# Gram matrices of a pairwise-attention kernel in two parts of 32 rows on eight tiles of TensorE

## What is computed

```
row, col = triu_indices(39, k=1)                 # 741 pairs of fields
ip     = x[:, row, :] * x[:, col, :]             # (B, 741, 64)
hidden = relu(ip @ W_w + b_w)                    # (B, 741, 64)
logits = hidden @ W_h + b_h                      # (B, 741)
a      = softmax(logits, axis=1)
y      = (sum over pairs of a * ip) @ W_p + b_p  # (B, 1)
```

## Time and profile before

| | us |
|---|---|
| median of 3 runs (1036.34 to 1036.84) | 1036.56 |
| the profiled execution | 1036.49 |
| its span in the profile | 1034.7 |
| PE busy | 1023.2 (99%) |
| DVE busy | 980.4 (95%) |
| ACT busy | 872.6 (84%) |
| POOL busy | 402.7 (39%) |

### The profile page before, as it was taken

One profiled execution on the slowest core, in us unless ns is written; L12 is line 12 of the kernel. 1 busy time (PEld: TensorE's weight loads), 2 busy tenths in 40 slices (PEclk: granted clock), 3 DMA queues, 4 the chain that ended last, 5 costly groups with the idle time before them and its releaser, 6 DMA issues.

```text
span 1034.7 us, 58749 instructions
## 1 busy us (share of the span) xinstructions
PE 1023.2 (99%) x24849; PEld 486.7 (47%) x24849; DVE 980.4 (95%) x550; ACT 872.6 (84%) x885; POOL 402.7 (39%) x326
## 2 busy tenths in 40 slices
PE   8999999999999999999999999999999999999997
PEld 3445454454544545454454544545445454454542
DVE  8999999999999999999999999999999999999992
ACT  6888888888888888888888888888888888888885
POOL 3644555333334333343424334233343333433331
PEclk9999999999999999999999999999999999999999
DMA  3242242422324133241421414214232242422312
GB/s 53 36 50 48 36 51 47 50 36 48 41 43 58 27 55 41 36 62 29 56 44 27 62 35 50 47 31 55 44 41 47 36 49 47 46 39 45 41 35 27
DMA packets 330745, 45.33 MB, mean 44 GB/s; under 512 B 330715, under 2 KB 330731, under 8 KB 330731
## 3 DMA queue, kind: packets, MB, share of 16 engines
q1 hardware_dynamic: 330411, 45.10, 30.7%
q10 hardware_dynamic: 320, 0.07, 0.0%
HBM read 26.59 MB, written 18.54 MB: 44 GB/s over the span
## 4 chain that ended last, share of the span: by engine, by line
PE 97%; DVE 2%; DMA 0%; issue 0%; ACT 0%; DVEq 0%; ACTq 0%
PE z L517 62%; PE logits L570 31%; PE z L506 5%; DVE prod L345 2%; DMA first_x_rows<-in_r_x_dram 0%; DVE x_wide L316 0%; PE logits L558 0%; DVE neg_max L354 0%; DVE weighted L362 0%; ACT exps L453 0%; PE z L497 0%; DVE x_wide L319 0%; DVE x_scaled L320 0%; PE z L640 0%; DVE x_wide L327 0%
## 5 line engine op out<-in xcount | busy, mean ns | idle before, releaser
L430 ACT ACTIVATE hidden<-z,b_col 128x988 f32<-128x988 f32 x768 | 803.9, 1084 | 132.2 <-PE z L517 127.5
L345 DVE TENSOR_TENSOR prod<-x_wide 128x2964 f32<-128x2964 f32 (+1 forms) x257 | 821.2, 3243 | 1.0 <-issue 0.2
L517 PE MATMUL z<-prod,w_tiles 64*32 64x494 f32 x12288 | 761.1, 576 | 1.4 <-DVE prod L345 0.7
L284 POOL COPY head_w<-head_cols 128x64 f32<-128x64 f32 x252 | 354.7, 1411 | 559.2 <-PE logits L570 559.2
L570 PE MATMUL logits<-hidden,head_w 64*32 64x371 f32 (+1 forms) x8192 | 440.6, 471 | 0.4 <-PE logits L570 0.4
L517 PEld LDWEIGHTS z<-prod,w_tiles 64*32 64x32 f32 x12288 | 260.5, 106 | 247.8 <-issue 223.0
L570 PEld LDWEIGHTS logits<-hidden,head_w 64*32 64x32 f32 x8192 | 179.8, 106 | 244.5 <-issue 229.2
L316 DVE STREAM_TRANSPOSE x_wide<-x_rows 128x1024 f32<-128x1024 f32 x63 | 78.4, 1245 | 24.5 <-PE z L506 20.9
L506 PEld LDWEIGHTS z<-x_wide,x_scaled 64*39 64x39 f32 x4096 | 44.8, 113 | 39.5 <-issue 39.5
L438 ACT COPY gram_out<-z 103x624 f32<-103x624 f32 x64 | 44.3, 692 | 17.4 <-PE z L506 17.4
L291 POOL COPY gram_out<-gram_out 103x304 f32<-103x304 f32 x64 | 39.4, 615 | 46.8 <-ACT gram_out L438 46.8
(11 more groups left out here) (29 smaller groups left out, 26.5 us busy)
## 6 DMA issues: line engine op xcount, KB each, us to landing
gram<-gram_out SPq DMA_DIRECT2D x256, 70.7 KB
x_rows<-in_r_x_dram SPq DMA_DIRECT2D x252, 64.0 KB
values<-gram SPq DMA_DIRECT2D x128, 46.3 KB, 3.5
x_rows<-in_r_x_dram SPq DMA_DIRECT2D x252, 14.0 KB
first_x_rows<-in_r_x_dram SPq DMA_DIRECT2D x2, 78.0 KB
first_x_rows<-in_r_x_dram SPq DMA_DIRECT2D x1, 156.0 KB
w_tiles<-in_L_rec_W_w_dram ACTq DMA_DIRECT2D x4, 16.0 KB, 2.8
head_cols<-in_L_rec_W_h_dram SPq DMA_DIRECT2D x4, 0.2 KB, 2.3
```

The costliest lines, as they stand in the source:

```text
L284: nc.gpsimd.tensor_copy(head_w[:, step % BLOCK_STEPS, :, :], head_cols[:, :, at:at + TILE]).then_inc(head_w_ready, 1)
L345: nc.vector.tensor_tensor(out, one, other, ALU.mult).then_inc(ready, 1)
L430: nc.scalar.activation(hidden[:, i, :, CHUNK * k:CHUNK * (k + 1)], z[:, slot_of(j), :, 0:CHUNK], ACT.Relu, bias=b_col[:, 0:1]).then_inc(z_ ...
L517: last = nc.tensor.matmul(z[col:col + TILE, slot_of(j), b, 0:CHUNK], w_tiles[row:row + D, col:col + TILE], prod[row:row + D, i, first:firs ...
```

## The change

The Gram matrix of an item is computed in two matmuls of 32 stationary columns in place of one of 39. Part 0 takes fields 0 to 31 as rows and columns 1 to 38 of x_wide; of it rows 0 to 19 are used. Part 1 takes fields 7 to 38 as rows and columns 20 to 57 of x_wide (which run over into the repeated fields); of it rows 13 to 31 are used, which are fields 20 to 38. With these two windows every row already has the columns that its pairs need, so nothing has to be repeated in `gram_out`. The eight tiles of 64 x 32 are the same as those of the chunks. A block then has 64 Gram matmuls of 38 columns in place of 32 of 39. ACT's copy takes all 128 partitions with 608 elements in place of 103 with 624. POOL's copy and the semaphore for it go, and SP waits for ACT's copy itself. In DRAM the rows have 38 entries; SP writes them in 8 DMAs a block, for u, h and part, in place of 4. The DVE memset of a corner of z at the start goes too, with TensorE's wait for it.

```diff
+    GCOLS = FIELDS - 1
+    CROSS_ROWS = FIELDS // 2 + 1
+    GRAM_PARTS = ((0, 1, 0, CROSS_ROWS, 0),
+                  (FIELDS - TILE, CROSS_ROWS, CROSS_ROWS - (FIELDS - TILE), FIELDS - CROSS_ROWS,
+                   CROSS_ROWS * GCOLS + CROSS_ROWS - 1))
+    GRAM_BATCH = FIELDS * GCOLS + CROSS_ROWS
...
-        gram_out = sb("gram_out", [P, 2, 2, ROW_DUOS, WIDE])
+        gram_out = sb("gram_out", [P, 2, 2, ROW_DUOS, GCOLS])
...
-        GRAM_DMAS = 4
+        GRAM_DMAS = 8
...
             def write_gram(v, slot):
-                sp.wait_ge(gram_wrapped, v + 1)
+                sp.wait_ge(z_read, ITEMS * v + place("gram") + 1)
                 for u in range(2):
                     for h in range(2):
-                        at = (h ^ u) * D
-                        sp.dma_start(gram_blocks[h, u, :, bass.ds(v, 1), :, :],
-                                     gram_out[at:at + FIELDS, slot, u, :, :]).then_inc(gram_written[slot], 16)
+                        for part, (_, _, skipped, rows, base) in enumerate(GRAM_PARTS):
+                            at = (h ^ u) * D + part * TILE + skipped
+                            first = gram_blocks[h, u, base:base + 1, bass.ds(v, 1), :]
+                            lines = bass.AP(first.tensor, first.offset, [[GCOLS, rows], first.ap[-1], [1, GCOLS]])
+                            sp.dma_start(lines, gram_out[at:at + rows, slot, u, :, :]).then_inc(gram_written[slot], 16)
...
                         bands = bass.AP(first.tensor, first.offset,
-                                        [first.ap[0], [WIDE + 1, FIELDS], [1, OFFSETS]])
+                                        [first.ap[0], [GCOLS + 1, FIELDS], [1, OFFSETS]])
...
-            def wrap_gram(v):
-
-                pool.wait_ge(z_read, ITEMS * v + place("gram") + 1)
-                rows = gram_out[0:ROWS, v % 2, :, :, :].rearrange("p u d w -> p (u d) w")
-                nc.gpsimd.tensor_copy(rows[:, :, FIELDS:WIDE], rows[:, :, 0:OFFSETS]).then_inc(gram_wrapped, 1)
...
-            nc.vector.memset(z[TILE:D, GRAM_SLOT, 0, QUADS * FIELDS:XCOLS], 0.0).then_inc(z_cleared, 1)
...
-                nc.scalar.copy(gram_out[0:ROWS, slot, :, :, 0:FIELDS],
-                               z[0:ROWS, GRAM_SLOT, :, 0:XCOLS].rearrange("p u (d f) -> p u d f", f=FIELDS)
+                nc.scalar.copy(gram_out[:, slot, :, :, :],
+                               z[:, GRAM_SLOT, :, 0:ROW_DUOS * GCOLS].rearrange("p u (d f) -> p u d f", f=GCOLS)
                                ).then_inc(z_read, 1)
...
             def gram_matrices(v):
                 for d in range(ROW_DUOS):
-                    for u in range(2):
-                        for h in range(2):
-                            row, col, duo = h * D, (h ^ u) * D, u * ROW_DUOS + d
-                            last = nc.tensor.matmul(z[col:col + FIELDS, GRAM_SLOT, u, FIELDS * d:FIELDS * (d + 1)],
-                                                    x_scaled[row:row + D, duo, :], x_wide[row:row + D, duo, 0:FIELDS],
-                                                    start=True, stop=True, tile_position=(row, col))
+                    for part, (field, column, _, _, _) in enumerate(GRAM_PARTS):
+                        for u in range(2):
+                            for h in range(2):
+                                row, col, duo = h * D, (h ^ u) * D + part * TILE, u * ROW_DUOS + d
+                                last = nc.tensor.matmul(z[col:col + TILE, GRAM_SLOT, u, GCOLS * d:GCOLS * (d + 1)],
+                                                        x_scaled[row:row + D, duo, field:field + TILE],
+                                                        x_wide[row:row + D, duo, column:column + GCOLS],
+                                                        start=True, stop=True, tile_position=(row, col))
                 last.then_inc(z_ready, 1)
...
-            pe.wait_ge(z_cleared, 1)
```

More of the change, by code:

```diff
@@ L107, in bass_pairwise_attention_pooling @@
     x_rows_dram = x.rearrange("(v p h) f (e d) -> h e f v p d", v=BLOCKS, h=2, e=2)
-    gram = nc.dram_tensor("gram", [BATCHES, FIELDS, WIDE], fp32, kind="Internal").ap()
-    gram_blocks = gram.rearrange("(v u p h) i w -> h u i v p w", h=2, v=BLOCKS, u=2)
-    gram_rows = gram.rearrange("(t q h) i w -> h q t (i w)", h=2, q=QUADS)
+    gram = nc.dram_tensor("gram", [BATCHES, GRAM_BATCH], fp32, kind="Internal").ap()
+    gram_blocks = gram.rearrange("(v u p h) w -> h u w v p", h=2, v=BLOCKS, u=2)
+    gram_rows = gram.rearrange("(t q h) w -> h q t w", h=2, q=QUADS)
     y_rows_dram = y.rearrange("(g c) o -> g (c o)", g=GROUPS)
@@ L155, in bass_pairwise_attention_pooling @@
         x_rows_zeroed = sem("x_rows_zeroed")
-        z_cleared = sem("z_cleared")
         w_loaded = sem("w_loaded")
@@ L170, in bass_pairwise_attention_pooling @@
         x_scaled_ready = sem("x_scaled_ready")
-        gram_wrapped = sem("gram_wrapped")
         gram_written = [sem(f"gram_written{i}") for i in range(2)]
@@ L229, in load_values @@
                         at = 32 * q + GROUP_STEPS * h
-                        first = gram_rows[h, q, bass.ds(GROUP_STEPS * g, GROUP_STEPS), 1:2]
+                        first = gram_rows[h, q, bass.ds(GROUP_STEPS * g, GROUP_STEPS), 0:1]
                         bands = bass.AP(first.tensor, first.offset,
-                                        [first.ap[0], [WIDE + 1, FIELDS], [1, OFFSETS]])
+                                        [first.ap[0], [GCOLS + 1, FIELDS], [1, OFFSETS]])
                         sp.dma_start(values[at:at + GROUP_STEPS, 0:PAIRS].rearrange(
@@ L296, in _ @@
                 nc.gpsimd.tensor_copy(head_w[:, step, :, :], head_cols[:, :, at:at + TILE]).then_inc(head_w_ready, 1)
-            wrap_gram(0)
             for step in range(BLOCK_STEPS, STEPS):
-                if step % BLOCK_STEPS == BLOCK_STEPS - 1:
-                    wrap_gram(step // BLOCK_STEPS)
                 place_heads(step)
```

## The result

The changed kernel takes 1063.86 us (median of 4 runs, 1063.15 to 1066.6) against 1036.7 before: 27.2 us more, ratio 1.0268 (95% interval 1.0256 to 1.028). The forecast was 1057.8 in a range of 1048 to 1067. The profiled execution took 1063.15 with a span of 1061.4, 26.7 more than before's 1034.7.

What follows compares the result with a forecast made beforehand. TensorE's own stream was taken as the bound (PE busy 99%). A loss of 0.335 us a block, vanished gaps included, gave 64 x 0.335 = +21.4 on 1036.49, so 1057.9, stated as 1057.8 us, range 1048 to 1067.

Steps and rivals of the forecast that it cites:

- The gaps go: Idle time around a block's Gram matrices, where TensorE changes tile size, vanishes: -0.31 us a block.
- A matmul each 0.0167 us: Hand-over limit: TensorE gets one float32 matmul each 0.0167 us at best, read from seven chunk matmuls behind `open_logits`.
- The window's limit of 0.0173: About 16 matmuls queued or under way in TensorE, each counted until complete: 0.277 / 16 = 0.0173 us a matmul.
- The last tile: Last tile of the chunk after the Gram matrices starts at 1.29 us in place of 0.955: +0.335 a block.
- The lower bound: With hand-over of 0.0167 us alone as the limit: +0.305 us a block, +19.5 us.
- "Nothing" for SP: SP's 4 more issues a block, 1.3 to 2.0 us, cost nothing; last values still in time at the end.
- The memset and its wait: nothing: Memset and its wait at the start lie before x arrives, so removing them changes nothing.
- The sum: Whole kernel: 1036.49 + 21.4 = 1057.9 us, given as 1057.8.
- Tile pace: Rival, chance 0.05: only the tiles set the Gram matmuls' pace, -0.31 us a block, -19.8 us, 1016.7.
- Starts at 0.0067: Rival, chance 0.06: record starts 0.0067 us apart set the Gram pace, 0.05 a block saved, -3.2 us, 1033.3.
- Gaps that stay: Rival, chance 0.04: gaps around the Gram matrices belong to short matmuls and stay, 0.645 a block, +41 us, 1077.8.
- Something behind TensorE late: Rival, chance 0.04: DVE's spread or ACT's copy is late, a chunk waits, 0.1 a block or more: 1064 to 1075.

Runs made afterwards that it cites:

- 6: Kernel before the change with 32 of 39 fields stationary in its 32 Gram matmuls, all blocks but the first: 1022.95 us (0.987).
- experiment 1: Changed kernel with only its 19-row writes split into 10 and 9 rows, 12 DMAs a block: 1060.99 us (1.0229).
- 4: Changed kernel with half the duos left out, 32 Gram matmuls a block, in all blocks but the first: 1028.65 us (0.9921).
- 5: Changed kernel with 8 moving columns in place of 38 in its 64 Gram matmuls, all blocks but the first: 1063.79 us (1.0266).
- the last kernel: Complete kernel with 40 Gram matmuls a block in place of the changed kernel's 64, GpSimd scaling seven fields, two 128-row writes a block: 1034.35 us (0.998).

## Why the prediction was right, point by point

- **The gaps go.** Right, and shown to be the tile size's (6). In full they are not gained, since the hand-over takes over; the sum had that in it.
- **A matmul each 0.0167 us.** Right, and the whole of the loss: 0.335 a block forecast, 0.328 measured; 17.0 ns a matmul by leaving 32 out, and no effect of the columns. That it follows from the starts of seven records at one place was the risk taken, and the pace held for the stream. That it held to 2% is luck: the times are read to 0.01 us, so (0.70 - 0.60) / 6 could have been anything from 0.015 to 0.018. The window's limit of 0.0173 was never seen to bind; the two are too near to be told apart here.
- **The last tile.** It was forecast to start 1.29 behind the half's end by the first tile; it is later still, but the half now starts as unevenly, and what counts is the difference between blocks. The two errors cancel.
- **The lower bound** has a slip: 1.255 - 0.955 is 0.300 a block and 19.2 us, not 0.305 and 19.5. It changes nothing in the range.
- **"Nothing" for SP** was the step that failed. It counted DMAs and their issue at the 0.33 to 0.50 us of the earlier trace rows, and took those of other row counts as equal. Behind a 19-row write an issue takes up to 2.6 us, and the last one lands late. It cost the end 3.6 us (4.68 of waiting against 1.04), in place of "still in time", and 2.9 of the median by experiment 1. In the kernel before a split into 20 and 19 rows cost 113.
- **"The memset and its wait: nothing"** left out the start as a whole. The first four blocks lose 2.05 beyond the matmuls. The pause of 0.55 and about 0.5 of later clock are in it; where the rest goes is open.
- **The sum.** 21.4 us for TensorE; measured 63 x 0.328 and the last block's, 21. The other 5.7 are the end and the start, 3.6 + 2.05. That 1063.86 still lies in the range is partly luck: it reached up to 1067 for ACT or DVE holding up a chunk, which did not happen, and not for a slow write or the start.
- **The rivals.** Tile pace: refuted by 4 and 5. Starts at 0.0067: the same, for the Gram records alone start within 1.21 us and not 0.86. Gaps that stay: refuted by the timeline. Something behind TensorE late: true only for the last read of values.

## What to carry to other kernels

Price small float32 matmuls by their number first: here 17 ns each, whether they had 8 or 38 moving columns and whether they ran on four or eight tiles. Fewer and wider ones paid, though only by 0.2% in a whole kernel. Packing work onto more tiles helps only while each matmul is long enough for the next to be handed over. Look at the row count of every DMA for its divisors: a split into 20 and 19 rows cost 113 us in a kernel where 26 and 13 cost nothing. And when one wait shows up in TensorE's stream, look at the granted clock behind it: about a third of those 113 us was work that took longer at the lower level.

## What the runs showed that was not expected

- Behind a write of 19 rows x 8 pieces of 152 bytes an issue takes 2.5 us in place of 0.3, and the last such write lands after 5.5, with a busy share of the DMA engines of 0.12 in place of 0.70.
- With 8 in place of 38 moving columns the 64 float32 matmuls of a block take the same time to 0.014 us.
- An uneven start of the tiles, once there, lasts through the 12 chunks and 8 halves that follow: each half between 515 and 535 us shows 0.90 in place of 0.82.
- GpSimd's scaling of 128 x 112 elements takes 3.86 us on average beside a busy VectorE, by its group in the last kernel:

```profile
L301 POOL TENSOR_SCALAR x_rest<-x_wide,wp_col 128x112 f32<-128x112 f32 x63 | 242.9, 3856 | 120.5 <-DVE x_wide L332 120.5
```
